# Attention block with its values kept on chip and its keys computed four steps ahead, in place of whole-batch staging through DRAM

## The reference

```python
q = (layernorm(x) @ Wq.T) * 32 ** -0.5            # B 16, L 224, H 16, D 32
k = ctx @ Wk.T                                    # S 750
v = ctx @ Wv.T
o = sigmoid(einsum('blhd,bshd->bhls', q, k))      # no softmax, no row sums
x = x + tanh(g_xattn) * (einsum('bhls,bshd->blhd', o, v) @ Wo.T)
h = gelu(tokens(layernorm(x)) @ w1[e] + b1[e])    # F 2048 per expert
x = x + tanh(g_ffn) * (h @ w2[e] + b2[e])
```

## Time and profile before

| | |
|---|---|
| median of three runs | 1877.3 us |
| profiled execution, first to last instruction (span) | 1868.1 us |
| what lies around the span, median minus span | 9.2 us |
| TensorE busy in the span | 1786.9 us (96%) |
| first scores; last batch's first scores; end of the batches | 54.8; 1144.6; 1227.6 us |
| experts, from 1227.6 us to the end | 640.5 us |
| wait of the heads for `v_sb` | 46.0 us in 18 waits |
| longest single wait of TensorE, at the start | 8.7 us |

### The profile page before, as it was taken

The page is one execution under the profiler, slowest core; times in us unless marked ns, Lnnn a source line. Parts: engine busy times, 40 slices in busy tenths (PEclk is TensorE's granted clock), DMA queues, the critical chain, the costliest instruction groups (busy, mean ns, idle before and its releaser), DMA issues.

```text
span 1868.1 us, 35544 instructions
## 1 busy us (share of the span) xinstructions
PE 1786.9 (96%) x12672; PEld 1527.1 (82%) x12672; DVE 692.1 (37%) x1320; ACT 774.4 (41%) x1004; POOL 268.9 (14%) x397
## 2 busy tenths in 40 slices
PE   7899999999999999999999998799999999999998
PEld 7678787887887787877877876589999999999997
DVE  5223323233232232233232331255453544545453
ACT  4444454444444443544444443533333333333331
POOL 2222122222221221222222221000000000000000
PEclk9899999999999999999999998899999999999999
DMA  7988879798898888898898988743543535343451
GB/s 243 220 219 234 218 225 231 205 252 210 222 247 205 229 230 210 223 247 198 243 243 196 246 216 199 181 142 114 169 133 108 174 111 158 125 149 132 124 169 41
DMA packets 239490, 356.82 MB, mean 191 GB/s; under 512 B 19536, under 2 KB 162000, under 8 KB 239440
## 3 DMA queue, kind: packets, MB, share of 16 engines
q1 hardware_dynamic: 205504, 246.61, 53.1%
q0 software_dynamic: 33936, 109.54, 18.0%
HBM read 245.65 MB, written 110.43 MB: 191 GB/s over the span
## 4 chain that ended last, share of the span: by engine, by line
PE 83%; DMA 12%; SPq 2%; ACT 1%; DVE 1%; issue 1%; POOLq 0%; DVEq 0%; ACTq 0%
PE fill_ps L468 34%; PE scores_ps L625 17%; PE fill_ps L607 17%; PE heads_ps L517 7%; DMA v_sb<-v_scr 7%; PE scores_ps L501 7%; DMA v_scr<-v_stage 2%; DMA q_st<-q_scr 2%; SPq L269 1%; PE fill_ps L567 1%; ACT v_stage L719 0%; SPq L339 0%; ACT probs L689 0%; DMA k_scr<-k_stage 0%; PE fill_ps L641 0%
## 5 line engine op out<-in xcount | busy, mean ns | idle before, releaser
L689 ACT ACTIVATE probs<-scores_ps 125x1792 f32<-125x1792 f32 x192 | 319.9, 1666 | 219.2 <-PE scores_ps L501 219.2
L607 PE MATMUL fill_ps<-wQ,wK 128*128 128x448 f32 x1536 | 331.2, 369 | 0.0
L625 PE MATMUL scores_ps<-ctx_hl,wV 128*128 128x448 f32 x1536 | 324.5, 367 | 0.8 <-ACT x1nT L723 0.8
L468 PE MATMUL fill_ps<-ctx_hl,wK 128*128 128x250 f32 x2304 | 306.0, 283 | 9.1 <-DVE wK L818 8.7
L607 PEld LDWEIGHTS fill_ps<-wQ,wK 128*128 128x128 f32 x1536 | 287.9, 189 | 27.1 <-issue 1.1
L625 PEld LDWEIGHTS scores_ps<-ctx_hl,wV 128*128 128x128 f32 x1536 | 287.0, 187 | 28.0 <-issue 0.9
L468 PEld LDWEIGHTS fill_ps<-ctx_hl,wK 128*128 128x128 f32 x2304 | 286.2, 192 | 14.9 <-issue 13.7
L468 PE MATMUL fill_ps<-wV,ctx_hl 128*125 128x512 f32 x1152 | 292.1, 402 | 0.0
L468 PEld LDWEIGHTS fill_ps<-wV,ctx_hl 128*125 128x125 f32 x1152 | 206.1, 185 | 77.2 <-issue 31.5
L517 PE MATMUL heads_ps<-probs,v_sb 125*32 125x224 f32 x3072 | 191.1, 368 | 46.9 <-DMA v_sb<-v_scr 46.0
L868 DVE TENSOR_TENSOR k_stage<-fill_ps,k_stage 128x250 fp32r<-128x250 f32 x192 | 79.9, 417 | 406.1 <-ACT k_stage L713 404.6
(11 more groups left out here) (78 smaller groups left out, 1201.8 us busy)
## 6 DMA issues: line engine op xcount, KB each, us to landing
k_st<-k_scr SPq DMA_DIRECT2D x192, 375.0 KB, 7.7
w_raw<-w_in SPq DMA_DIRECT2D x128, 512.0 KB, 4.4
k_scr<-k_stage POOLq DMA_DIRECT2D x192, 250.0 KB, 7.2
ctx_raw<-ctxT_in SPq DMA_DIRECT2D x48, 500.0 KB, 9.0
v_scr<-v_stage POOLq DMA_DIRECT2D x96, 250.0 KB, 6.2
v_sb<-v_scr SPq DMA_DIRECT2D x64, 375.0 KB
q_st<-q_scr SPq DMA_DIRECT2D x192, 112.0 KB, 8.5
q_scr<-q_stage POOLq DMA_DIRECT2D x64, 224.0 KB, 6.4
```

The costliest lines, as they stand in the source:

```text
L468: last = pe.matmul(out_, lhsT(kt, a), rhs(kt, c), start=(kt == 0 and t == 0), stop=(kt == KT - 1 and t == 2))
L607: last = pe.matmul(hid_ps[k][:, 0:T], w1[:, slot, a, kt, k * P:(k + 1) * P], xt[:, d, kt, :], start=(kt == 0 and t == 0), stop=(kt == KT - ...
L625: last = pe.matmul(y_ps[:, dt, 0:T], w2[:, slot, a, k, dt * P:(dt + 1) * P], hid_hl[:, slot, d, k, :], start=(c == 0 and k == 0 and t == 0 ...
L689: nc.scalar.activation(probs[0:ST, s % 2], scores_ps[0:ST, :, 0:2 * L], ACT.Sigmoid, scale=SCALE).then_inc(s_probs, 1)
```

## The change

Values. `v_sb` becomes [P, 2, 6, 512], two batches of whole values; ScalarE copies each V fill from PSUM straight into it. `v_stage`, `v_scr`, their stores and their loads are gone. `load_v`'s waits are gone with them.

Keys. `k_scr` and `q_scr` shrink to rings of 4 and 2 places. A K fill (one group, one third of the context) is stored, and gathered at once into one of four places of `k_st3`; fill i of batch b is for the step i + 4, that is, steps 8 to 11 make the keys of steps 0 to 3 of the next batch. Three gathers per fill, in rows of 1000 bytes (before: 3000).

Queries. Q 1, 2 and 3 are now fills of the batch that uses them: Q 1 in step 1 for step 3, Q 2 in step 4 for step 6, Q 3 in step 7 for step 9, and Q 0 in step 10 for step 0 of the next batch.

Heads. `heads` runs once per group, in steps 0, 3, 6 and 9, with 24 matmuls; `probs` has three places for it.

Order. There is no side A any more; all fills follow scores and heads. The layer norm of x1 is in steps 3 and 4, that of x in steps 11 and 0. The x residual is loaded in step 8, the next x in step 9; context thirds in steps 1, 2 and 7. In the prologue only four K fills, five V, one Q and T are done.

Rows. The inputs `ctxT`, the attention weights, `w1` and `w2` come in rows of 4000 or 4096 bytes per partition. Weights are staged in `probs`, `v_sb` and `k_stage` in place of buffers of their own.

```diff
-    FILL = [(0, "A", "T", 0), (0, "A", "T", 1), (0, "B", "K", 0),
-            (1, "A", "K", 1), (1, "B", "O", 0), (2, "A", "K", 2), (2, "B", "O", 1),
...
+    FILL = [(0, "K", 0), (0, "V", 5), (1, "Q", 1), (1, "K", 1), (1, "O", 0), (2, "K", 2), (2, "O", 1), (3, "K", 3),
+            (4, "Q", 2), (4, "K", 4), (5, "K", 5), (5, "U", 0), (5, "U", 1), (6, "K", 6), (7, "Q", 3), (7, "K", 7),
+            (7, "V", 0), (8, "T", 0), (8, "T", 1), (8, "K", 8), (8, "V", 1), (9, "K", 9), (9, "V", 2),
+            (10, "Q", 0), (10, "K", 10), (10, "V", 3), (11, "K", 11), (11, "V", 4)]
+    FILL_FIRST = [(0, "K", 8), (1, "K", 11), (2, "V", 0), (3, "V", 1), (4, "K", 9), (5, "V", 2), (6, "T", 0), (6, "T", 1),
+                  (7, "K", 10), (8, "Q", 0), (9, "V", 3), (10, "V", 4)]
...
+            def gather_k(b, i):
+                r = i % 4
+                alone(sp, s_k_st[r], 16 * (3 * b + 2 + i // 4))
+                alone(sp, s_scores, STEPS * b + i + 1)
+                for t, half in enumerate((HI, LO, HI)):
+                    sp.dma_start(k_st3[t * HD:(t + 1) * HD, r].bitcast(F32),
+                                 scr["k"][r, half].rearrange("(j p) s -> p j s", p=HD)).then_inc(s_k_in[r], 16)
+
+            def gather_q(b, i):
+                n, r = target(b, "Q", i), i % 2
+                alone(sp, s_q_st[r], 16 * (2 * n + i // 2 + 1))
+                alone(sp, s_scores, STEPS * n + 3 * (i - 2) + 3)
+                for t, half in enumerate((HI, HI, LO)):
+                    sp.dma_start(q_st3[t * HD:(t + 1) * HD, r].bitcast(F32),
+                                 scr["q"][r, half].rearrange("(j p) l -> p j l", p=HD)).then_inc(s_q_in[r], 16)
...
+            def body(b, h, par):
+                nh, npar = (h, 1) if par == 0 else (h + 1, 0)
+                for s in range(STEPS):
+                    if known(b, B - 1) and s == 2:
+                        expert_start()
+                    if not known(b, -1) and prepares(b) and s in (1, 2, 7):
+                        load_ctx(b + 1, nh, npar, {1: 0, 2: 1, 7: 2}[s])
+                    if s == 8 and attends(b):
+                        alone(sp, full["U"], 2 * b)
+                        load_x(x_res, b, s_xr_in)
+                    if s == 9 and prepares(b, 2):
+                        alone(sp, full["T"], nth("T", b, 1))
+                        load_x(x_ln[0:LT], b + 2, s_x_in)
+                    for kind, i in fills_at(b, s):
+                        if kind == "K":
+                            gather_k(b, i)
+                        if kind == "Q":
+                            gather_q(b, i)
...
+            def store_q(b, i):
+                n, r = target(b, "Q", i), i % 2
+                alone(pool, done["Q"], nth("Q", b, i))
+                alone(pool, s_q_in[r], 16 * COPIES * (2 * n + i // 2))
+                pool.dma_start(scr["q"][r].rearrange("h p l -> p h l"), q_stage[:, r].bitcast(F32)
+                               ).then_inc(s_q_st[r], 16)
+
+            def store_k(b, i):
+                r = i % 4
+                alone(pool, done["K"], nth("K", b, i))
+                alone(pool, s_k_in[r], 16 * COPIES * (3 * b + 1 + i // 4))
+                pool.dma_start(scr["k"][r].rearrange("h p s -> p h s"), k_stage[:, r].bitcast(F32)
+                               ).then_inc(s_k_st[r], 16)
...
             def scores(b, s):
+                mt = s // 3
+                slot, r = mt % 2, s % 4
+                if s % 3 == 0:
+                    pe.wait_ge(s_q_in[slot], 16 * COPIES * (2 * b + mt // 2 + 1))
+                pe.wait_ge(s_k_in[r], 16 * COPIES * (3 * b + s // 4 + 1))
                 at(pe, s_probs, STEPS * b + s)
...
+            def heads(b, par, mt):
+                if mt == 0:
+                    pe.wait_ge(done["V"], 6 * (b + 1))
+                at(pe, s_o_lo, KT * b + mt)
+                pe.wait_ge(s_probs, STEPS * b + 3 * mt + 3)
+                for pair in range(3):
+                    for t in range(2):
+                        for j in range(HEADS):
+                            last = pe.matmul(heads_ps[j * HD:(j + 1) * HD, 0:L],
+                                             v_sb[0:ST, par, 2 * pair + t, mt * P + j * HD:mt * P + (j + 1) * HD],
+                                             probs[0:ST, pair, j, t * L:(t + 1) * L],
+                                             start=(pair == 0 and t == 0), stop=(pair == 2 and t == 1))
+                    last.then_inc(s_av, 1)
...
+            def body(b, h, par):
+                for s in range(STEPS):
+                    if attends(b):
+                        scores(b, s)
                     if s == 0 and follows(b):
-                        heads(b - 1, STEPS - 1)
-                    if s > 0 and attends(b):
-                        heads(b, s - 1)
+                        heads(b - 1, 1 - par, KT - 1)
+                    if s > 0 and s % 3 == 0 and attends(b):
+                        heads(b, par, s // 3 - 1)
+                    for kind, i in fills_at(b, s):
...
+            def leave_v(b, par, i):
+                n, place = target(b, "V", i), par if i == 5 else 1 - par
+                act.wait_ge(full["V"], nth("V", b, i))
+                at(act, s_av, STEPS * (n - 1))
...
+                nc.scalar.copy(v_sb[0:ST, place, i, :], fill_bank(b, "V", i)[0:ST, :]).then_inc(done["V"], 1)
...
+                    if follows(b) and s in (3, 4):
+                        ln_x1(b, *((0,) if s == 3 else (1, 2)))
+                    if attends(b) and follows(b) and prepares(b) and s == 0:
+                        ln_x(b + 1, 1, 2)
+                    if attends(b) and prepares(b, 2) and s == 11:
+                        ln_x(b + 2, 0)
```

More of the change, by code:

```diff
@@ L70, in flamingo_block @@
[L70 to L74, removed]
+    assert T == NB * L and TT == LT and NB == 2 and KT == 4 and T <= 512 and C % 2 == 0 and C >= 4 and E >= 3
@@ L86, in known, with fills @@
     def known(b, value):
         return isinstance(b, int) and b == value
[L89 to L95, removed]
+    def fills(b):
+        if known(b, -1):
+            return FILL_FIRST
+        if known(b, 0):
+            return [f for f in FILL if f[1] not in "OU"]
+        if known(b, B - 1):
+            return [f for f in FILL if f[1] in "OU" or (f[1] in "KQ" and 0 < f[2] < 8) or f[1:] in (("K", 0), ("V", 5))]
+        if known(b, B):
+            return [f for f in FILL if f[1] in "OU"]
+        return FILL
@@ L97, in bank_of, with fills_at, target, nth @@
+    def fills_at(b, s):
+        return [(k, i) for t, k, i in fills(b) if t == s]
     def bank_of(b, kind, i):
         return (BANK_FIRST if known(b, -1) else BANK)[kind, i]
+    def target(b, kind, i):
+        return {"K": b + (i + 4) // STEPS, "V": b + (i != 5), "Q": b + (i == 0), "T": b + 1}.get(kind, b - 1)
+    def nth(kind, b, i):
+        if kind == "K":
+            return K_FIRST[i] if known(b, -1) else STEPS * b + 4 + i + 1
+        return {"V": 6, "Q": KT, "T": 2, "O": 2, "U": 2}[kind] * target(b, kind, i) + i + 1
@@ L105, in follows, with prepares @@
         return not isinstance(b, int) or b > 0
[L107 to L114, removed]
+    def prepares(b, ahead=1):
+        return not isinstance(b, int) or b + ahead < B
     def own(eng):
@@ L328, in load_xt @@
                     alone(sp, s_ctx_lo, 3 * B)
-                    for r in range(2):
-                        alone(sp, s_v_st[r], 16 * 3 * B)
                     alone(sp, s_x1nT_st, 16 * NB)
@@ L477, in bank_free @@
                     return
-                todo = [(k, j) for _, _, k, j in fill_of(b, prep, out_)]
+                todo = [(k, j) for _, k, j in fills(b)]
                 mine = todo.index((kind, i))
@@ L504, in scores @@
                 last.then_inc(s_scores, 1)
-            def heads(b, s):
-                mt, pair = s // 3, s % 3
-                slot = mt % 2
-                if pair == 0:
-                    pe.wait_ge(s_v_in[slot], 16 * (2 * b + mt // 2 + 1))
-                    at(pe, s_o_lo, KT * b + mt)
-                pe.wait_ge(s_probs, STEPS * b + s + 1)
-                for t in range(2):
-                    for j in range(HEADS):
-                        last = pe.matmul(heads_ps[j * HD:(j + 1) * HD, 0:L],
-                                         v_sb[:, slot, 2 * pair + t, j * HD:(j + 1) * HD],
-                                         probs[0:ST, s % 2, j, t * L:(t + 1) * L],
-                                         start=(pair == 0 and t == 0), stop=(pair == 2 and t == 1))
-                last.then_inc(s_av, 1)
@@ L568, in fill, with body @@
                 last.then_inc(full[kind], 1)
-            def body(b, prep, out_, ahead):
+            def body(b, h, par):
                 for s in range(STEPS):
@@ L597, in hidden @@
                 if known(e, 0) and c == 0:
-                    if k == 0:
-                        pe.wait_ge(s_x1, 2 * (B - 1))
-                    else:
-                        pe.wait_ge(done["U"], 2 * (B - 1))
```

(20 more changed lines are left out.)

385 lines of the change are left out of this document (171 added, 214 removed), and 6 rows, old and new, of the table FILL.

## The result

The changed kernel takes 1958.3 us (median of four runs, 1950.7 to 1960.7) against 1876.1 for the kernel before: a ratio of 1.043 (95% interval 1.038 to 1.048), 4.3% slower. The forecast was 1928, 2.7% slower, with a range of 1860 to 2000.

What follows compares the result with a forecast made beforehand. TensorE bound the kernel, plus one exposed DMA round trip of a value tile. A batch: 68.4 + 5.3 + 2.3 + 1.0 = 77.0 us; total 59 - 16 + 8 = +51, span 1919, plus 9.2: 1928 us, range 1860 to 2000.

Steps and rivals of the forecast that it cites:

- TensorE's work: Fills, scores and heads of a batch: 69.5 us before, 68.4 after, as four heads' visits of 2.4 us save 1.1.
- The wait for Q 2: Scores of step 6: Q 2 ready 12.1 us after step 4 starts, due at 6.9; TensorE waits 5.3 us every batch.
- The estimate of 2.5 and 2.3: Q 2's store and each gather by the Trainium skill's fixed cost plus bandwidth, in us; wait about 3.2 us.
- The layer norm's 1.6 us: Second part of x1's layer norm in step 4 ends 1.6 us late for the U fills, hidden under Q 2's wait.
- The clock: Half speed after Q 2's wait of 5.3 us: 2.3 us lost a batch, ends 0 and 3.
- The other queries: Waits for Q 1, Q 3 and Q 0: 0.3, 0.5 and 0.2 us, together 1.0 a batch, ends 0 and 6.
- last batch and epilogue: 83.0 us before; 19 us more fills, mostly in time spent waiting, and two Q waits of 7.6 us: +8.
- The 9.2 us: Median of the runs, 1877.3 us, above the span of 1868.1; put on top of the forecast span of 1919.
- The keys: K 3, filled in step 3 for step 7, needs 10.1 us and has 11.7; K 2 and K 4 over 14.
- ScalarE holds no step back: The shortest step, 3.1 us, is more than ScalarE's 0.2 + 0.87 + 1.67.
- Short round trips: Rival, chance 0.18: store plus gather under 5.4 us, Q 2 3.5 late, clock mostly stays; 1860 us.
- Loaded queues: Rival, chance 0.22: queues loaded as before, store plus gather 8 us, Q 2 6.4 late, 2.8 of clock; 1990 us.

Runs made afterwards that it cites:

- experiment 5: The kernel before with the values part alone: two batches of whole values in v_sb, no v_scr loads or stores, batch loop unrolled by two; 1832.7 us, ratio 0.975.
- experiment 2: The changed kernel with the whole layer norm of x1 at the end of step 2, Q 2 left in step 4; 1970.4 us, ratio 1.053.
- experiment 10: experiment 9 with the first two context thirds loaded in steps 2 and 5 in place of 1 and 2; 1843.9 us, ratio 0.982.
- experiment 6: The changed kernel with the context loaded in rows of 1000 bytes again, all else as changed; 1960.3 us, ratio 1.044.
- experiment 3: The changed kernel with Q 2 filled in step 2 and the layer norm of x1 at the end of step 2; 1847.0 us, ratio 0.984.
- experiment 8: experiment 4 with K 8 ahead of step 8's T fills, context splits in steps 5, 6, 8, third context load in step 6; 1787.3 us, ratio 0.951.
- experiment 1: The changed kernel with Q 2 filled in step 2 in place of step 4; 1860.2 us, ratio 0.991.
- experiment 4: experiment 3 with Q 1, Q 3 and Q 0 one step earlier too (steps 0, 6, 9); 1849.2 us, ratio 0.985.
- experiment 7: The changed kernel with Q 2 filled in step 3 and the layer norm of x1 in step 2; 1880.6 us, ratio 1.000.
- experiment 9: experiment 3 with K 8 first in step 8 and the last context split in step 8 in place of 9; 1833.1 us, ratio 0.978.

## Why the prediction was right, and where it was not

The likeliest case came true: the wait moved from the values to Q 2, and it costs more than the change saves. By its steps:

**TensorE's work, 68.4 us a batch**: right. Less what half speed cost, TensorE is busy 68.3 us a batch in the changed kernel, against 69.5 in experiment 5, where the heads' visits are still 12. The heads' visit of 24 took 2.41 us at full clock (2.4).

**The wait for Q 2, 5.3 us late**: right in place and nearly in size. Over the 14 batches step 6 starts 11.1 us after step 4 in place of 6.9, 4.2 late, with 4.0 us idle; without the layer norm in the way (experiment 2) the wait is 4.9. Store and gather, taken as 3.5 and 3.3 us, were 3.0 and 2.9 on average; the rest of the path came within 0.2 us. The estimate of 2.5 and 2.3, with a wait of 3.2, was too low. The layer norm's 1.6 us beneath it was 1.9, and worth nothing while Q 2 is late, as said (experiment 2).

**The clock, 2.3 us a batch**: too low. In the 14 batches the clock is at the lower level for 122.9 us in 18 stretches; TensorE is busy in 102.6 of them, so half speed cost 51.3 us, 3.7 a batch. The falls came in every batch and, in four, twice, the other one after Q 1's wait. The price had also been read too low: in the row with 5.8 us of waiting the clock is low from 1154.3 to 1164.6, of which 5.5 us and not 4.6 lie behind the wait. And the wait of 3.5 us that cost nothing was no rule: in batches 1 to 14 of the kernel before, the clock fell after or in seven of the nine waits of over 2 us.

**The other queries, 1.0 us together**: too low. They are 23.3 + 2.7 + 1.9 = 27.9 us in 14 batches, 2.0 each, nearly all of it Q 1's. I named the context load ahead of it, but gave it 0.3 us: Q 1's store took 5.4 us on average and not 3.5, and experiment 10 shows that the load decides.

**Left out**: V 1 waits 1.2 us for the low half of T to leave a bank, K 10 0.6 us for the context's low half; 25.7 us in 14 batches. The prediction says that nothing else in TensorE's work changes. Fills that follow each other without heads in between wait for their banks, and this I did not go through.

In the sum: 68.3 + 4.0 + 3.7 + 2.0 + 1.8 = 79.8 us a batch and not 77.0, 14 x 2.8 = 39 us. The whole miss of the span is 40 us (1959.0 against 1919), but the two are this close only because four smaller errors cancel. The last batch's first scores stand at 1149.3 us in the kernel before, not at 1144.6, which is step 11 of batch 14:

```profile
1145.48 1.57 PE L468 MATMUL fill_ps<-ctx_hl,wK 128*128 128x250 f32 x12
...
1149.31 1.03 PE L501 MATMUL scores_ps<-q_st,k_st 96*125 96x224 f32 x8
1150.27 0.96 PE L517 MATMUL heads_ps<-probs,v_sb 125*32 125x224 f32 x16
```

The last batch fills no keys any more, so its first scores are the second ones here. With that, forecast and measured:

| | forecast | measured |
|---|---|---|
| start | -16 | -14.5 |
| batch 0 | even | +4.3 (74.1 to 78.4) |
| batches 1 to 14 | +59 | +97.0 (1020.4 to 1117.4) |
| last batch and epilogue | +8 | +12.3 (78.3 to 90.6) |
| experts | 0 | -8.2 (640.5 to 632.3) |
| span | +51 | +90.9 |

That the last stretch came out at 91 as forecast is luck: its length before had been taken 4.7 us too long. The experts' 8 us were costed at nothing. They are there in every run with the change's layout, experiment 6 too (632.3), and not in experiment 5 (642.1), which leaves the rows of weights as they were; TensorE is idle for some 6 us of them in either, and what makes its busy time 8 us shorter stays open.

The 9.2 us that I put around the span were wrong too: in every execution that has both, the time lies 1.7 us above the span (1960.7 and 1959.0 here), so the profiled execution of before was some 6 us shorter than the median; that hid 7 us of the miss.

**The keys**: four steps ahead were enough, as worked out; no wait for `k_st` in the batches of the changed kernel. K 3 is ready 9.5 us after its fill ends (10.1 forecast). This rests on steps of the present length: see experiments 3 and 8.

**ScalarE holds no step back**: true of the changed kernel. Once Q 2 is out of step 4, it holds back step 5 by 0.45 us (experiments 1, 3, 4 and 7 to 10).

**Rivals.** Short round trips: store and gather together were 5.6 to 6.3 us for Q 2, in no batch under 5.4, and waits of 4.0 us in two parts did cost the clock. Loaded queues: wrong as to load (DMAs 58% busy, from 88% before), and right for moments: Q 1's store takes 5.1 us with a context load beside it and 3.0 without (experiments 9 and 10).

**What the parts are worth.** Values on chip: 48 us off the kernel before (experiment 5). The place of Q 2: 98 us on the changed one (experiment 1). Longer context rows: nothing (experiment 6). How far the larger heads' visits pay by themselves was not run; the rows give 4 x 0.26 us a batch. Rows of weights were not tried alone; the experts' 8 us may be theirs.

## What to carry to other kernels

When data takes a detour through memory, hold the age of each item against the length of the steps in between, not against their number: for Q 2 two steps were 6.9 us here and the detour 11.0; for K 3 four steps were 12.1 us and the detour 9.6 (experiment 8). The average load of the queues says little about it: a Q store and a Q gather each took less than half the time of before, and the kernel became slower, since it now needed them at once. And after removing one wait, go through the whole order again for the fills or splits that the wait, or the item moved, had covered (experiments 4 and 9). A moved item also makes one step longer and another shorter, and so gives or takes time from the others' detours (Q 1 in experiments 1 and 7, the keys in experiment 3).

## What was not expected of the hardware

The length of a wait is a poor guide to what it costs in clock. In experiment 4 TensorE waits 2.0 to 2.1 us for K 10 at the same place of all 14 batches: the granted clock fell after five of these waits and stayed at 1.00 after nine. In the changed kernel it fell around step 6 of all 14 batches, with an idle time of 1.9 us, 0.9 to 1.5 us of work and one of 1.7 to 2.5 us: to 0.72 over 12 us in batch 7. The second idle time is not needed for it: in batches 7, 10, 11 and 13 the clock fell before that began. The 14 waits of 1.3 us in experiment 1 left it at 1.00, and so did one of 3.5 us before. What decides it was not tested.

And a context load that needs 4.2 to 5.5 us itself, issued 0.4 us ahead of a Q store on another queue, goes with a store of as much as 7.1 us, where 2.6 is seen without one. On average over 14 batches the store takes 5.1 us with such a load beside it and 3.0 without (experiments 9 and 10, which differ in the place of two loads alone).
